# Two routers of eight experts with their weights in the array and the tokens moving

## The reference

```python
# L2: one expert for each token
logits = xt @ Wr + br                       # xt [1250, 512], Wr [512, 8], br [8]
probs = jax.nn.softmax(logits, axis=-1)
G, idx = jnp.max(probs, axis=-1), jnp.argmax(probs, axis=-1)
# L3: two experts for each token, at most `capacity` tokens for each expert
probs = jax.nn.softmax(xf @ router_w + router_b, axis=-1)
_, topk_idx = jax.lax.top_k(probs, TOP_K)
```

## Time and profile before

| | |
|---|---|
| time, median of 3 runs | 3237.43 us (3237.39 to 3237.93) |
| the profiled execution's own time | 3236.85 us |
| its span | 3235.0 us |
| TensorE busy, clock granted on the mean | 2629.9 us (81%), 0.895 of full |
| VectorE, ScalarE busy | 1690.7 us (52%), 1039.2 us (32%) |
| router products of L2 | 2127.84 to 2150.11 us |
| router products of L3 | 3050.82 to 3073.84 us |

### The profile page before, as it was taken

The page is one execution under the profiler, slowest core; times in us unless marked ns, Lnnn a source line. Parts: engine busy times, 40 slices in busy tenths (PEclk is TensorE's granted clock), DMA queues, the critical chain, the costliest instruction groups (busy, mean ns, idle before and its releaser), DMA issues. The chain is left out here.

```text
span 3235.0 us, 40132 instructions
## 1 busy us (share of the span) xinstructions
PE 2629.9 (81%) x12039; PEld 1818.8 (56%) x12040; DVE 1690.7 (52%) x3404; ACT 1039.2 (32%) x2287; POOL 278.9 (9%) x273
## 2 busy tenths in 40 slices
PE   5778779957999976999598789958877579998874
PEld 2334346545787744665274466656635367777552
DVE  7898821255888725444534432331133378886343
ACT  2555520023667710111301122211111247776110
POOL 0000000000000002443000000002300000000031
PEclk9999989978999987999798899959979789998777
DMA  3000041011000027896502400034250110000344
GB/s 106 26 16 16 16 114 45 17 45 31 20 19 19 13 58 239 304 304 200 132 14 119 90 14 13 1 114 147 69 124 9 47 36 20 19 16 16 102 126 110
DMA packets 113648, 238.20 MB, mean 74 GB/s; under 512 B 32600, under 2 KB 33960, under 8 KB 112230
## 3 DMA queue, kind: packets, MB, share of 16 engines
q10 hardware_dynamic: 42608, 116.92, 12.7%
q1 hardware_dynamic: 46582, 91.71, 9.6%
q0 software_dynamic: 24320, 27.90, 3.0%
HBM read 189.78 MB, written 52.58 MB: 75 GB/s over the span
## 5 line engine op out<-in xcount | busy, mean ns | idle before, releaser
L309 PE MATMUL ps<-onehot_src,onehot_dst 125*128 x1140 | 257.6, 358 | 81.3 <-ACT stage_hi L367 36.6
L1171 DVE TENSOR_REDUCE mx<-ps 125x1 f32<-125x500 f32 (+1 forms) x480 | 274.1, 589 | 56.6 <-PE ps L941 40.1
L1066 ACT ACTIVATE probs_hi<-ps 125x500 fp32r<-125x500 f32 (+1 forms) x480 | 254.9, 531 | 123.4 <-DVE probs_lo L1123 82.2
L1123 DVE TENSOR_TENSOR probs_lo<-x,probs_hi 125x1250 fp32r<-125x1250 f32 x160 | 241.1, 1507 | 34.7 <-ACT x L1068 31.2
L1068 ACT ACTIVATE x<-ps 125x500 f32<-125x500 f32 (+1 forms) x480 | 257.5, 537 | 0.0
L1815 DVE COPY yb<-ps 78x512 f32<-78x512 f32 (+1 forms) x100 | 68.8, 688 | 321.4 <-PE ps L1752 321.4
L265 DVE TENSOR_SCALAR onehot_src<-iota,src_f 125x1250 f16 x380 | 206.1, 542 | 37.5 <-PE ps L309 27.8
L309 PEld LDWEIGHTS ps<-onehot_src,onehot_dst 125*128 x1140 | 105.7, 101 | 210.1 <-issue 156.2
L1752 PE MATMUL ps<-w2s,hT 128*78 128x512 f32 (+1 forms) x480 | 216.4, 597 | 1.9 <-ACT hT L1777 1.9
L941 PE MATMUL ps<-K_hi_lo,Q_hi_twice 128*125 128x500 f32 (+1 forms) x480 | 181.1, 383 | 22.8 <-DVE mx L1171 17.6
L949 PE MATMUL ps<-Q_hi_twice,K_hi_lo 128*125 128x500 f32 (+1 forms) x480 | 178.9, 373 | 17.8 <-ACT Q_lo_max L1056 5.1
(11 more groups left out here) (378 smaller groups left out, 4847.0 us busy)
## 6 DMA issues: line engine op xcount, KB each, us to landing
room<-in_L_ffn_w_p ACTq DMA_DIRECT2D x63, 512.0 KB, 5.5
w2s<-in_L_ffn_w ACTq DMA_DIRECT2D x63, 512.0 KB, 7.1
G<-c_spill ACTq DMA_DIRECT2D x2, 5859.4 KB
tv<-in_L_ffn_tv_W_p SPq DMA_DIRECT2D x2, 4096.0 KB
w_spill<-weight_rows ACTq DMA_DIRECT2D x10, 585.9 KB
c_spill<-CT ACTq DMA_DIRECT2D x1, 5859.4 KB
slabs<-w_spill SPq DMA_DIRECT2D x10, 585.9 KB
w1s<-in_L_ffn_w_p ACTq DMA_DIRECT2D x5, 1024.0 KB, 4.8
```

The source lines that it names most:

```text
L309: mm_ = pe.matmul(ps[:, 3 * half + c, 0:cn], ohd[:, slot, :].rearrange("p o n -> p (o n)"), ohs[:, slot, c0:c0 + cn].rearrange("p o n -> p ...
L1066: act.activation(PH[:, t % 2, c0:c0 + cn], ps[0:P, ST + n, 0:cn], ACT.Exp, scale=SCALE).then_inc(p_hi, 1)
L1123: v.tensor_tensor(PL[:, t % 2, :], PT[:, t % 2, :], PH[:, t % 2, :].bitcast(fp32), ALU.subtract)\
L1171: v.tensor_reduce(mx[:, t, n:n + 1], ps[0:P, SQ + cc % 2, 0:cn], AX.X, ALU.max)\
```

## The change

In routers with a bias the operands trade places. `wr` [128, 8] of each chunk stands in the array and `yT` moves, 500, 500 and 250 tokens at a time, so that the logits come out as [8, 1250] in banks 5, 6 and 7. ScalarE copies each of the three pieces to a new tile `LT` and adds the bias as a column on the way (`br` is now loaded as [8, 1]). Ten transposes of [8, 125] on TensorE write what the old code had in banks 0 and 1. All twelve products are issued first, then the ten transposes, each behind a wait for the piece it reads. L0's router has no bias and keeps the old code. Two semaphores are new.

```diff
@@ route
+        if br is not None:
+            LT = sb("logits_T", [E_, N])
...
+        columns_done, columns_out = sem("columns_done"), sem("columns_out")
@@ tensor
+                if br is not None:
+                    for n, (c0, cn) in enumerate(CH):
+                        for c in range(C):
+                            mm = pe.matmul(ps[0:E_, 5 + n, 0:cn], wr[:, c, :], yT[:, c, c0:c0 + cn], start=(c == 0),
+                                           stop=(c == C - 1))
+                        mm.then_inc(columns_done, 1)
                 for t in range(T):
                     o = ps[0:P, t // PB, E_ * (t % PB):E_ * (t % PB) + E_]
-                    for c in range(C):
-                        mm = pe.matmul(o, yT[:, c, P * t:P * t + P], wr[:, c, :], start=(c == 0),
-                                       stop=(c == C - 1 and br is None))
                     if br is not None:
-                        mm = pe.matmul(o, k.ones[0:1, 0:P], br, start=False, stop=True)
+                        pe.wait_ge(columns_out, P * t // 500 + 1)
+                        mm = pe.transpose(o, LT[:, P * t:P * t + P], k.ident[0:E_, 0:E_])
+                    else:
+                        for c in range(C):
+                            mm = pe.matmul(o, yT[:, c, P * t:P * t + P], wr[:, c, :], start=(c == 0),
+                                           stop=(c == C - 1))
                 mm.then_inc(logit_done, 1)
@@ scalar
+                if br is not None:
+                    for n, (c0, cn) in enumerate(CH):
+                        act.wait_ge(columns_done, n + 1)
+                        act.activation(LT[:, c0:c0 + cn], ps[0:E_, 5 + n, 0:cn], ACT.Identity, bias=br)\
+                            .then_inc(columns_out, 1)
                 act.wait_ge(shifted, 1)
                 act.activation(W[:, :, :], L[:, :, :], ACT.Exp).then_inc(exps, 1)
@@ transformer (and the same in l2_ffn)
-        b2r, wr, br = sb(ctx, "b2r", [E_, D]), sb(ctx, "wr", [128, C, E_]), sb(ctx, "br", [1, E_])
+        b2r, wr, br = sb(ctx, "b2r", [E_, D]), sb(ctx, "wr", [128, C, E_]), sb(ctx, "br", [E_, 1])
...
-                  + ([(br[:, :], row(a[pre + "router_b"]))] if bias else []))
+                  + ([(br[:, :], a[pre + "router_b"].rearrange("(e o) -> e o", o=1))] if bias else []))
```

More of the change, by code:

```diff
@@ L2320, in l2_ffn @@
         xn, xT = sb(ctx, "xn", [P, T, D]), sb(ctx, "xT", [128, C, N])
-        b2r, wr, br = sb(ctx, "b2r", [E_, D]), sb(ctx, "wr", [128, C, E_]), sb(ctx, "br", [1, E_])
-        norm_rows(nc, k, x, xn, xT, have_stats=True, beside=[(wr[:, :, :], kchunks(a["L2_ffn_Wr"])), (br[:, :], row(a["L2_ffn_br"])),
+        b2r, wr, br = sb(ctx, "b2r", [E_, D]), sb(ctx, "wr", [128, C, E_]), sb(ctx, "br", [E_, 1])
+        norm_rows(nc, k, x, xn, xT, have_stats=True, beside=[(wr[:, :, :], kchunks(a["L2_ffn_Wr"])), (br[:, :], a["L2_ffn_br"].rearrange("(e o) -> e o", o=1)),
                                             (b2r[:, :], a["L2_ffn_b2"])])
```

## The result

The changed kernel takes 3216.49 us (median of 7 runs, 3202.72 to 3220.93) where the kernel before, timed beside it, takes 3240.23 us (7 runs, 3237.39 to 3247.96): a ratio of 0.9924, with a 95% interval of 0.991 to 0.9939. That is 23.7 us less; the sum of the prediction was 24.0 us less.

What follows compares the result with a forecast made beforehand. TensorE's router products in L2 and L3 were taken as the bound; saving 12.4 and 11.6 us, together 24.0, from 3236.85 gave 3212.85, plus 0.58 for the median: 3213.4 us. Own range 3209 to 3218, reaching to 3227.

Steps and rivals of the forecast that it cites:

- the sum of the prediction: Both routers: L2 9.9 us against 22.27, L3 11.4 against 23.02; 12.4 and 11.6 less, together 24.0.
- Products: Wide products in each router: 24 passes, 16 of 0.420 and 8 of 0.210 us, 8.4 us at full clock.
- Which clock: Wide products in L2 and L3: full clock taken, 8.4 us; half clock, 16.8 us, kept as the other bound.
- the other support: Rows with 64 columns or 64 partitions standing and some 500 moving: 0.43 and 0.48 us each, cited for full clock.
- Busy time and the clock: New router stretch: the skill's throttle by recent TensorE busyness gives full clock, 8.4 us; weighed less than the rows.
- The start: Start of the products: L2 at full clock, L3 3 us at half costing 1.5 us, bounds 0 and 5.2 us (2.6).
- Transposes, copies, table: After the products: ten transposes 1.5 us at full clock; ScalarE's third copy covered by 0.1 us, table load by 0.3.
- the cover: ScalarE's third copy ends by 0.8 us, under eight transposes of 0.9: covered by 0.1 us; uncovered, up to 0.8.
- the rival that is 0.5 us late in each router: Table load before the exponential: ScalarE must empty first, exponential 0.5 us late in each router, 3214.4 us; chance 0.07.
- its signs of being wrong: Clock 0.50 in the router window, ScalarE's copy delaying the ninth transpose, gap before the exponential, later stages over 3 us longer.
- half clock in part: One router's clock falls or rises late: 5 us more at half cost 2.5 each, 3216 to 3222 us; chance 0.13.

Runs made afterwards that it cites:

- the run with 128 partitions: Changed kernel with 24 more unused products (48 passes) in each router, fed from 128 partitions; stretches 29.97 us in L2 and L3, time 3263.2 us.
- the runs with 8 and 32 partitions: Changed kernel with 24 more unused products in each router, fed from 8 or 32 partitions; L2 stretch 46.78 us in both, times 3291.7 and 3295.29 us.

## Why the prediction was right

**Products.** 8.4 us were predicted and 2137.31 - 2128.83 = 8.48 measured; a record lasts 580 ns against "some 590".

**Which clock.** Right, but partly for a reason that doesn't hold. The prediction set L0's router against L1760 and read from it that a narrow side of columns keeps the clock, since that router ran at 1.00. The window was cut where the router ends, and the clock fell 0.9 us behind it; the same passes in L2 fell after 2.4 us. That row said that 9 us of such work may pass at full clock, and nothing on what it does for long., the other support, say little more. L320's passes stand singly among other products, and the 0.43 us is the length of one record. L1760's 20 passes from 64 partitions are one stretch of 9.57 us at full clock, which falls 2.4 us behind them (1534.7 us). The rows that bear on a long stream are L2's experts in the kernel before, 85 us at full clock with 125 or 128 partitions fed (timeline rows, the last a window):

```profile
1522.78 9.57 PE L1760 MATMUL ps<-b2r,gateT 64*125 64x512 f32 x20
...
2187.00 8.79 PE L1743 MATMUL ps<-xbT,w1s 128*128 128x125 f32 x64
2195.62 7.03 PE L1752 MATMUL ps<-w2s,hT 128*125 128x512 f32 x16
...
2190.20:2275.20 85.00, 74.88 (x426) 52.76 (x425) 12.63 (x20) 11.33 (x40) 23.74 (x28) 1.00 0.42 141
```

They have wide standing sides, so for a narrow one the prediction had no row. It chose rightly, in part by luck, and the run with 128 partitions shows the choice for 30 us.

**Busy time and the clock.** The Trainium skill (TensorE: Matmul & The Clock Gate, Part 1) lets the clock follow how busy TensorE has been. The prediction weighed it less than the rows. In the runs with 8 and 32 partitions TensorE was busy for all 46.6 us and at 0.50 for 33.7 and more of them, so the traces don't agree: busy time as the records have it doesn't give these falls.

**The start.** In L2 at full, as the earlier trace rows had it. In L3 3 us at half were predicted and 3.2 measured, so 1.6 us against 1.5. It was 3.08 to 3.22 us in seven profiles with the new form in L3, and none in the run with 48 more passes from 128 partitions; never the 5.2 us of the earlier trace rows.

**Transposes, copies, table.** The transposes with their tail took 1.37 us against 1.5. The third copy began 0.11 us into the transposes (0.25 predicted) and ended 0.57 us into them, at 2137.88 (0.8 predicted); nothing waited, and the cover was 0.3 us where the prediction had 0.1. The load ended at 2139.18, and the exponential began at 2139.56 when VectorE was done: covered by 0.38 us against 0.3, and 0.88 us behind the first copy against 0.89. No drain shows: ScalarE's load stands 0.02 us behind its copy, so the rival that is 0.5 us late in each router is out, and so are the 1.38 us that the Trainium skill (ScalarE: Activation LUTs, What ACT_TABLE_LOAD costs) puts to it.

**The sum.** 9.85 and 11.43 us against 9.9 and 11.4. The profile's span came out 3.7 us above the sum (3214.7 against 3235.0 less 24.0), nearly all of it the 3.5 us between the routers, where the prediction had added nothing and allowed 3. So one of its signs of being wrong, stages behind that take over 3 us more, did come; it came with 7.4 us more at half clock, and not with more work. The median of the runs is 3.1 us above the forecast, inside its own range of 3209 to 3218. It lies in the range of "half clock in part" (3216 to 3222) as well; what decides between them are the windows, 1.00 in L2 and 3.2 us at 0.50 in L3. That the medians differ by 23.7 us, so near to 24.0, is partly luck, since seven runs of the changed kernel scatter over 18 us.

**One number off.** The prediction priced all 100 old passes alike, at 0.22 us. 80 cost 0.207, and the bias's 20 cost 0.30 with what they add to their neighbours. The sum didn't use it, since the whole stretch went. It matters to one who would only move the bias to ScalarE and leave the products: that would save 6 us a router at half clock, not 4.4.

**Where the gain is from.** Half of L3's 23.02 us is 11.5, so at full clock the old form would have taken little more than the new one's 9.85 us. Some 11 of L2's 12.4 us are the clock, and 1 to 2 the shorter work. This is worked out and not run: no stream with 125 columns standing and 8 or 64 moving kept the clock in L2 or L3.

What stays open is where between 32 and 128 partitions the clock holds; 64 held it for 9.57 us, where 8 and 32 lost it 3 to 4 us in. The columns that move seem to weigh too: with 128 partitions fed and 125 to 128 columns standing, the clock fell with 8 and with 64 moving and held in L2's experts with 125 and 512. Those are other stages, and no run took the moving side from 64 to 500 under 125 columns in the router itself.

## What to carry to other kernels

Where a product moves few columns over a wide standing side, the standing side is its price, here 0.11 us a pass at full clock and 0.21 at half for 125 columns, and such a stream also lost the clock here. Let the narrow side stand and the wide one move, and where it is as narrow as these 8 columns, put four products side by side. Don't take a short stretch at full clock as evidence for a long one: 9 us of these passes ran at full clock in one place, and the same passes fell after 2.4 us in another. Where the clock moves totals by several microseconds from run to run, judge a small edit by its stretch in the trace, and its total by many runs.

## What was not expected of the hardware

- 20 passes of one partition, 125 columns standing and 8 moving, cost 0.30 us each at half clock, while those of 128 partitions cost 0.207. The smaller product is dearer: 0.25 us from start to start, and the rest at the passes ahead of it. No row here says why.
- 32 partitions bring the clock down like 8: 46.78 us in L2 and 49.22 us in L3 with either.
- Four fp32 products in strips of 8 columns run at once: 8.48 to 2.22 us.
- A router's stretch in unchanged code was 22.27 and 21.00 us in two executions, by the moment at which the clock fell.
